# One chip, one core: the heads' skip term as a diagonal product, with moved gate exponentials, state order, fill products in routing and weight pieces between expert blocks

## What is computed

```python
x = x + mamba2(gate(x, f, f, w0, u0, cond))      # state-space layer, 16 heads of 64, state 128
x = x + experts(gate(x, f, f, w1, u1, cond))     # 8 experts, each token goes to two
x = x + attention(gate(x, f, f, w2, u2, cond))   # 16 heads, 4 groups, causal
x = x + ffn(gate(x, f, f, w3, u3, cond))         # 11 slices of 128
```

```python
y = (Y_diag + Y_off) + x_conv * D_skip     # per head and token; D_skip one number per head
y = y * silu(z)
y = y * rsqrt(mean(y * y) + eps) * norm_w
return y @ out_proj.T
```

## Time and profile before

| | |
|---|---|
| median of three runs | 2651.27 us |
| profiled execution | 2644.21 us, its span 2642.5 us |
| mean granted clock of TensorE | 0.938 |
| TensorE busy | 2266.7 us, 86% |
| VectorE busy | 1902.3 us, 72% |
| ScalarE busy | 943.0 us, 36% |
| GpSimd busy | 684.0 us, 26% |
| DMA | 142.19 MB, 54 GB/s |

### The profile page before, as it was taken

The page is one execution under the profiler, slowest core; times in us unless marked ns, Lnnn a source line. Parts: engine busy times, 40 slices in busy tenths (PEclk is TensorE's granted clock), DMA queues, the critical chain, the costliest instruction groups (busy, mean ns, idle before and its releaser), DMA issues.

```text
span 2642.5 us, 33318 instructions
## 1 busy us (share of the span) xinstructions
PE 2266.7 (86%) x10335; PEld 1713.3 (65%) x10352; DVE 1902.3 (72%) x2875; ACT 943.0 (36%) x1948; POOL 684.0 (26%) x545
## 2 busy tenths in 40 slices
PE   0788879979877599988957889999999998999998
PEld 0344444444446478767746777887887877788886
DVE  8888898889885866566635557787787776566665
ACT  2243342442341332333324334444444444322222
POOL 5433434324342334333331102212212210000000
PEclk9998989989986799989978999999999999999999
DMA  5000001001023331343141100001001101000001
GB/s 201 16 32 32 32 16 48 16 16 48 16 78 143 132 111 64 111 151 111 52 183 33 32 0 32 32 0 40 32 0 40 48 16 62 26 24 24 24 12 64
DMA packets 50502, 142.19 MB, mean 54 GB/s; under 512 B 4768, under 2 KB 4768, under 8 KB 46064
## 3 DMA queue, kind: packets, MB, share of 16 engines
q1 hardware_dynamic: 31872, 89.89, 9.6%
q10 hardware_dynamic: 12864, 32.81, 3.4%
q0 software_dynamic: 5680, 18.62, 2.3%
HBM read 106.95 MB, written 34.34 MB: 53 GB/s over the span
## 4 chain that ended last, share of the span: by engine, by line
PE 43%; issue 29%; POOL 9%; DVE 8%; POOLq 5%; ACT 3%; DMA 2%; ACTq 1%; SPq 0%; DVEq 0%
PE bank L340 9%; PE bank L341 9%; PE bank L342 9%; PE bank L2242 4%; PE bank L2243 4%; PE bank L2244 4%; PE bank L2205 3%; POOLq L486 2%; POOL g_v L487 2%; POOL g_v L494 2%; PE bank L2305 1%; POOLq L512 1%; DVE mw L1739 1%; PE bank L2237 1%; POOLq L509 1%
## 5 line engine op out<-in xcount | busy, mean ns | idle before, releaser
L2079 PE MATMUL bank<-um,w_in 128*128 128x512 f32 x576 | 260.3, 606 | 7.0 <-DVE lm L1463 6.7
L2079 PEld LDWEIGHTS bank<-um,w_in 128*128 128x128 f32 x576 | 108.8, 194 | 136.8 <-issue 125.5
L340 PE MATMUL bank<-u_hi,aw_hi 128*128 (+1 forms) x384 | 159.0, 414 | 14.6 <-DVE k_lo L1830 10.9
L1096 ACT ACTIVATE probs<-bank,nmx 128x128 f32<-128x128 f32 (+3 forms) x256 | 131.8, 527 | 91.0 <-DVE nmx L1849 91.0
L341 PE MATMUL bank<-u_lo,aw_hi 128*128 (+1 forms) x384 | 152.2, 396 | 0.0
L342 PE MATMUL bank<-u_hi,aw_lo 128*128 (+1 forms) x384 | 152.1, 396 | 0.0
L1103 ACT ACTIVATE pt_hi<-bank 128x512 fp32r<-128x512 f32 (+1 forms) x192 | 93.9, 526 | 156.7 <-PE bank L2205 156.7
L2205 PE MATMUL bank<-ident,probs 128*128 128x128 f32 x640 | 93.9, 278 | 54.8 <-DVE pt_lo L1864 35.2
L340 PE MATMUL bank<-u_hi,fw_hi 128*128 128x512 f32 x352 | 136.9, 389 | 0.0
L341 PE MATMUL bank<-u_lo,fw_hi 128*128 128x512 f32 x352 | 136.9, 389 | 0.0
L342 PE MATMUL bank<-u_hi,fw_lo 128*128 128x512 f32 x352 | 136.9, 389 | 0.0
(11 more groups left out here) (383 smaller groups left out, 6260.5 us busy)
## 6 DMA issues: line engine op xcount, KB each, us to landing
m_stage<-in_moe SPq DMA_DIRECT2D x21, 1024.0 KB, 6.4
y_slot<-m_o ACTq DMA_DIRECT2D x39, 256.0 KB, 2.4
g_v<-in_fT SPq DMA_DIRECT2D x18, 512.0 KB, 3.4
gates<-g_v SPq DMA_DIRECT2D x18, 512.0 KB, 2.8
f_stage<-in_ffn SPq DMA_DIRECT2D x11, 768.0 KB, 4.3
u_g<-gates SPq DMA_DIRECT2D x8, 1024.0 KB, 5.7
aw_in<-in_att SPq DMA_DIRECT2D x4, 1280.0 KB, 6.0
w_in<-in_w_in ACTq DMA_DIRECT2D x1, 4640.0 KB, 17.0
```

What stands on the lines that cost most here:

```text
L340: nc.tensor.matmul(out, hi_w, hi_x, start=start, stop=False)
L1096: A(probs[:, h % 2, PR_AT[qb]:PR_AT[qb] + w], S_[bk][:, c0:c0 + w], ACT.Exp, bias=nmx[:, h % 2, qb:qb + 1], scale=SCALE, accum_out=rsum[:, ...
L2079: mm = M(dst[:], w_in[:, k, c0:c0 + P], um[:, k, :], start=(k == 0), stop=(k == KC - 1))
```

## The change

Seven edits: `d_diag` is built on ScalarE in the setup and used on TensorE; VectorE's chain of a pair has other operations; block states and state sums have a new common order; gate exponentials and VectorE's clamp and scans of `third` move by one pair; TensorE issues fill products into a spare bank during routing; the weight splits of an expert are cut into pieces that stand between the steps of the next block, in a branch of their own; and the waits are adapted.

```diff
-            sb("pad_x", [P, D_IN], F32, s)
+            d_diag = sb("d_diag", [P, XC, P], F32, s)
...
+        AT_PREFIX, AT_POSITION, AT_ROWS = 38, 47, 51
...
+        def keep_busy(n):
+            for _ in range(n):
+                nc.tensor.matmul(SPARE[:].rearrange("p (a l) -> p a l", a=TB), ident_b[:],
+                                 causal_b[:].unsqueeze(1).to_broadcast([P, TB, P]), start=True, stop=True)
...
+        STATE_ORDER = [(0, 0), (0, 1), (1, 0), (1, 1), (0, 2), (1, 2)]
...
+            for j in range(XC):
+                A(d_diag[:, j, :], ident[:], ACT.Copy, scale=col("d_skip", j)).then_inc(setup_act, 1)
...
-                    if j == 1:
+                    if j == 2:
                         gate(mamba_pair(b, 2), 1)
-                    if j == 6:
+                    if j == PAIRS - 1:
                         gate(mamba_pair(b, 3), 0)
...
                     with act.If(flags[q] != 0):
                         e = act.value_load(...)
                         act.wait_ge(dn_done, FIRST + j)
-                        split_hi(e, e % 2)
-                    up_tanh(j + 1, (q + 1) % 3)
-                if not (last and q >= 1):
-                    u_hi_copy(j + 2)
+                        split_hi(e, e % 2, (0,))
+                        up_tanh(j + 1, (q + 1) % 3)
+                        split_hi(e, e % 2, (1,))
+                        if not (last and q >= 1):
+                            u_hi_copy(j + 2)
+                        split_hi(e, e % 2, (2,))
+                    with act.Else():
+                        up_tanh(j + 1, (q + 1) % 3)
+                        if not (last and q >= 1):
+                            u_hi_copy(j + 2)
...
-                    i = (TB - 1) * half + tb
+                    i = STATE_ORDER.index((half, tb))
...
-                for half in range(2):
-                    for tb in range(TB - 1):
-                        state_sum(tb, half)
+                for half, tb in STATE_ORDER:
+                    state_sum(tb, half)
...
                     step.inc(V.tensor_tensor(ej[:, P:T], YO[:, P:T], ej[:, P:T], ALU.mult))
-                    V.scalar_tensor_tensor(xj, xj, col("d_skip", j), YD[:], ALU.mult, ALU.add).then_inc(y_read, 1)
+                    dve.wait_ge(zs_done, PAIRS * b + j + 1)
+                    step.inc(V.tensor_tensor(xj[:, 0:P], YD[:, 0:P], zs[:, j, 0:P], ALU.mult))
                     step.wait()
+                    V.tensor_tensor(xj[:, P:T], YD[:, P:T], ej[:, P:T], ALU.add).then_inc(y_read, 1)
                     dve.wait_ge(y_read, PAIRS * b + j + 1)
-                    step.inc(V.tensor_tensor(xj[:, P:T], xj[:, P:T], ej[:, P:T], ALU.add))
-                    step.wait()
-                    dve.wait_ge(zs_done, PAIRS * b + j + 1)
-                    V.tensor_tensor(xj, xj, zs[:, j, :], ALU.mult).then_inc(y_done, 1)
+                    V.tensor_tensor(xj[:, P:T], xj[:, P:T], zs[:, j, P:T], ALU.mult).then_inc(y_done, 1)

                     if j == 0:
                         clamp(third, 0)
-                    elif j == 1:
+                    elif j == 2:
                         clamp(third, 1)
-                    elif j < 4:
-                        scans(third, j - 2)
+                        scans(third, 0)
+                    elif j == 3:
+                        scans(third, 1)
...
+            def next_inner(j, q, last):
+                inner(j + 1, (q + 1) % 3)
+                if not (last and q >= 1):
+                    select(j + 2, (q + 2) % 3)
+                    u_lo_split(j + 2)
...
-                        split_lo(e, e % 2)
-                    glu(j + 1, (q + 1) % 3)
-                    inner(j + 1, (q + 1) % 3)
-                if not (last and q >= 1):
-                    select(j + 2, (q + 2) % 3)
-                    u_lo_split(j + 2)
+                        split_lo(e, e % 2, (0,))
+                        glu(j + 1, (q + 1) % 3)
+                        split_lo(e, e % 2, (1,))
+                        next_inner(j, q, last)
+                        split_lo(e, e % 2, (2,))
+                    with dve.Else():
+                        glu(j + 1, (q + 1) % 3)
+                        next_inner(j, q, last)
...
                 to_tokens(7)
-                pe.wait_ge(xdt_done, XC * b + 7)
-                block_state(0, 2)
                 pe.wait_ge(xdt_done, XC * (b + 1))
-                for tb in range(TB - 1):
-                    block_state(1, tb)
+                for half, tb in STATE_ORDER[2:]:
+                    block_state(half, tb)
...
                 for j in range(PAIRS):
-                    pe.wait_ge(m_ready, 2 * (PAIRS * b + j + 1))
                     if j:
                         pe.wait_ge(y_read, PAIRS * b + j)
+                    M(YD[:], d_diag[:, j, :], xa[:, j, :], start=True, stop=False)
+                    pe.wait_ge(m_ready, 2 * (PAIRS * b + j + 1))
                     for hh in range(2):
                         for tb in range(TB):
                             M(YD[...], xdt[...],
-                              lm[:, j % 2, hh, tb * P:(tb + 1) * P], start=True, stop=True)
+                              lm[:, j % 2, hh, tb * P:(tb + 1) * P], start=False, stop=(tb == TB - 1))
...
+            pe.wait_ge(ob_read, KC * BATCH + 1)
...
                     if a >= 3:
+                        keep_busy({3: 12, 7: 16}.get(a, 0))
                         pe.wait_ge(ut_copied[(a - 3) % 2], (a - 3) // 2 + 1)
                     for kc in range(KC):
                         mm = transposed(UT[a % 3][:, kc * P:(kc + 1) * P], uf1[:, b, kc, o])
                     mm.then_inc(ut_T, 1)
+                    if a >= 3:
+                        keep_busy(2)
...
+            keep_busy(10)
             pe.wait_ge(route_vec, MASK_READY)
...
+            for at in (AT_PREFIX, AT_POSITION, AT_ROWS):
+                pe.wait_ge(dve_step, DVE_MAMBA * BATCH + at)
+                keep_busy(8)
             pe.wait_ge(route_vec, ONEHOT_READY)
...
             mm.then_inc(route_mm, 1)
+            keep_busy(8)
...
             pe.wait_ge(route_vec, TAB_READY)
+            keep_busy(12)
             inputs_T(0, 0, 0)
```

More of the change, by code:

```diff
@@ L326, in network @@
         BC = SM, EB
-        UT, LGP = bank[4:7], bank[7]
+        UT, LGP, SPARE = bank[4:7], bank[7], bank[0]
+        AT_PREFIX, AT_POSITION, AT_ROWS = 38, 47, 51
         UG, UL, DN, TP = bank[0:3], bank[3:6], bank[6], bank[7]
@@ L971, in u_hi_copy, with split_hi @@
                 A(bu_hi[:].rearrange("p k t -> p (k t)"), TP[:], ACT.Copy).then_inc(bu_hi_ready, 1)
-            def split_hi(e, slot):
-                for p in range(M_PIECES):
+            def split_hi(e, slot, pieces=range(M_PIECES)):
+                for p in pieces:
                     act.wait_ge(m_staged[p], 16 * (e + 1))
@@ L1531, in state_sum @@
                     if tb:
-                        dve.wait_ge(state_done, 2 * (TB - 1) * b + i)
+                        dve.wait_ge(state_done, 2 * (TB - 1) * b + STATE_ORDER.index((half, tb - 1)) + 1)
                         step.inc(V.tensor_tensor(state[:, tb, o].rearrange("p (h d) -> p h d", h=8),
@@ L1677, in _ @@
             each(V.tensor_reduce(nb[:, 0, :], cmp_, AX.X, ALU.add))
+            assert route.n == AT_PREFIX, route.n
             each(V.tensor_tensor_scan(nb[:, 1, :], ones[:, 0:E], nb[:, 0, :], 0.0, ALU.mult, ALU.add))
@@ L1687, in _ @@
                 each(V.tensor_reduce(posf[:, 0, k, :], rtmp[:], AX.X, ALU.add))
+            assert route.n == AT_POSITION, route.n
             each(V.tensor_scalar(posf[:, 1], posf[:, 0], 63.5, 1.0 / P, ALU.subtract, ALU.mult))
@@ L1700, in _ @@
                                       ALU.is_equal))
+            assert route.n == AT_ROWS, route.n
             each(V.tensor_tensor(oh_j[:], choices(1, NBLK), rconst("iota", NBLK).unsqueeze(1).to_broadcast([P, 2 * NT, NBLK]),
@@ L2161, in _ @@
                 to_tokens(7)
-                pe.wait_ge(xdt_done, XC * b + 7)
-                block_state(0, 2)
                 pe.wait_ge(xdt_done, XC * (b + 1))
-                for tb in range(TB - 1):
-                    block_state(1, tb)
+                for half, tb in STATE_ORDER[2:]:
+                    block_state(half, tb)
                 pe.wait_ge(ct_ready, b + 1)
                 for j in range(2):
-                    pe.wait_ge(state_done, 2 * (TB - 1) * b + (TB + j))
+                    pe.wait_ge(state_done, 2 * (TB - 1) * b + STATE_ORDER.index((1, j)) + 1)
                     sums(j)
@@ L2172, in _ @@
                 pe.wait_ge(bc_copied, 2 * TB * (b + 1))
+                pe.wait_ge(setup_act, 4 + 2 * KC + 2 * XC)
                 for j in range(PAIRS):
-                    pe.wait_ge(m_ready, 2 * (PAIRS * b + j + 1))
                     if j:
                         pe.wait_ge(y_read, PAIRS * b + j)
+                    M(YD[:], d_diag[:, j, :], xa[:, j, :], start=True, stop=False)
+                    pe.wait_ge(m_ready, 2 * (PAIRS * b + j + 1))
```

(1 more changed line is left out.)

## The result

The changed kernel took 2612.83 us (median of four runs, 2612.03 to 2615.82) where the kernel before took 2651.59 beside it: a ratio of 0.9857, 95% interval 0.984 to 0.9874. The forecast was 2614. The span of the profiled execution fell from 2642.5 to 2610.2 us.

A forecast was written before the change was run, and what follows sets the result against it. It took VectorE's order and its waits to set the pair loop, with neither TensorE nor VectorE alone bounding the state-space stage. State-space 15, routing 7 and experts 15 sum to 37 us off 2651.3: median 2614, range 2594 to 2634.

The forecast's parts named there:

- The pair loop's term: State-space stage: shorter VectorE chain and moved gate exponentials gain 3.8 us per sequence, 15 us in all (4 to 26).
- its new wait for TensorE: Pair loop: VectorE idles 6.4 us for TensorE at pairs without gate work and pair 0; net of 1.9 before, -4.5.
- The collision: Pair loop: moved clamp and scans, and pair 0's shorter chain, run beside GpSimd's products, costing 2.0 us per sequence.
- I take 3.8: From loop to sequence: of 4.2 us gained, 3.8 remain, mostly where TensorE waited 2.09 for the next sequence's step sizes.
- Routing: Fill products bring TensorE to full clock; nine token tiles take 1.71 us each for 2.45; gain 7 us.
- the losing case: Routing: if the clock stays down despite the fills, a tile takes 3.3 us, a loss of 7.7.
- Rival A: Routing: the fills do not hold the clock, -7.7 for +6.9, total gain 22, median 2629; chance 0.17.
- The expert term: Expert switches: weight pieces cut between the next block's steps let TensorE start earlier; gain 15 us (7 to 24).
- I expect the clock to stay ... 6: Experts: at three of five isolated switches idle under 2 us keeps the clock, about 2 us each, 6.
- Rival B: Pair loop: the diagonal at half clock eats the gain; stage gains 0 to 4, total 24, 2627; chance 0.15.
- D: Skip term has no effect, waits move to the next sequence's start; 22 to 26 left; chance counted within B's 0.15.
- C: Slower: the diagonal on every pair's path costs 57 us over 32 pairs, net +35, 2686; chance 0.02.

The follow-up runs named there:

- run 1: Changed kernel with VectorE's old four operations per pair and no diagonal product, the moved gate work and state order kept: 2618.62 us.
- run 2: Changed kernel with gate exponentials, clamps, scans and block-state order as in the kernel before, the diagonal product kept: 2638.28 us.
- Runs 1 and 3: run 1, and the changed kernel with only the old order of the block states, gate moves and diagonal kept: the latter 2610.45 us.
- run 6: Changed kernel without the two fill products inside each routing tile, all other fills kept: 2612.38 us.
- run 7: Changed kernel with all three expert weight pieces copied and subtracted ahead of tanh and gate product, as before the change: 2620.57 us.
- run 8: Changed kernel with the first two expert weight pieces ahead of tanh and gate product, the third behind the input split: 2602.22 us.
- run 10: On top of run 8, 34 fill products ahead of attention's first combine and 30 behind its first query projection: 2604.07 us.
- run 11: The changed kernel once more, unaltered, on the same chip as a repeat of run 8: 2609.19 us.

## Why the prediction was right, and where it was not

**The pair loop's term was too low (3.8 a sequence forecast, 6.9 measured in the third).** The working of the loop itself held as a sum: 4.2 forecast, 58.9 to 54.6 = 4.3 measured, but the parts differ, and that they cancel is luck. In the second sequence VectorE's busy time in the loop fell by 1.4 us (50.0 to 48.6) where 5.2 - 2.0 = 3.2 was forecast, and its idle time by 3.0 (8.8 to 5.8) where 5.5 - 4.5 = 1.0 was: its new wait for TensorE, put at 6.4, was 2.5. The waits for ScalarE were worth their 5.5: gate moves and state order alone shorten the loop by 5.8, and 0.2 of these waits is left then (run 1); with the diagonal 2.3 to 2.4 stay. The diagonal was to give 5.2 - 4.5 = 0.7 in the loop; it costs 1.5 to 1.7 there (VectorE's wait for TensorE is 7.3 with the diagonal alone and 1.9 in the kernel before), and gives 1.9 (alone) to 2.8 (with the moves) ahead of the next loop. The collision was there too: the scans L449 take 5.7 us for 4.7, beside GpSimd. The step that failed is the next one, "I take 3.8", which let the wait for step sizes in the next sequence eat part of the gain and counted nothing else in front of the loop. That wait barely moved (2.09 to 1.82), and the part ahead of the sums became 2.6 shorter. Two things are in it: the state order, 0.7 to 0.8 as forecast, which I had counted inside the loop; and TensorE at full clock in the first block states, 1.94 us at a granted clock of 1.00 where the kernel before took 3.37 at 0.55 for the same four records. In the kernel before:

```profile
524.90 3.37 PE L2155 MATMUL bank<-state,b_tok 128*128 128x512 f32 x4
```

and in the changed kernel:

```profile
511.53 1.94 PE L2182 MATMUL bank<-state,b_tok 128*128 128x512 f32 x4
```

In the last three sequences these records take 3.2 to 3.6 us in both profiles of the kernel before and in run 2, and 1.9 to 2.0 in all nine profiles with the changed kernel's code. Runs 1 and 3 have both: 1.9, 3.2 and 2.8 without the diagonal, 3.1, 1.9 and 1.9 with the old state order, and the part ahead of the sums goes with it (91.5, 93.1 and 92.8; 92.6, 91.0 and 91.0). The idle time right ahead, 2.4 us, is the same in all of them. So in these sequences full clock was seen only with the gate moves, and every time only with all parts together; why stays open. This time ahead of the loop is what the step left out.

**Routing was right in size and mechanism**: 7.9 and 7, tiles of 1.71, and 3.3 us in tiles at half clock ahead of them, the number of the losing case, which cost nothing, because ScalarE's next copy of a transpose waits for a store until 805.44. Rival A fell, and run 6 shows that without the two fills in each tile the clock falls as it says, at a price of 2.1 us and not A's 14.6 (four of the nine tiles still run at full clock, and none has fills to pay for): the trace's rows at 0.50 were good evidence, and with the two fills in each tile the clock held at 1.00 all the same.

**The expert term was too high (15; 11.0 by run 7, about 6 over all profiles).** Isolated switches gave 14.3, more than the 11 forecast, though 3.9 of it lies in the first block, whose length varies. "I expect the clock to stay ... 6" failed: TensorE idles 1.86 us and the blocks behind gain 3.3 together, one of them losing. The single-block expert cost 8.5 for 7, and the two blocks behind it returned 3.0, not 5.2: -5.5 for -1.8. The first price of the new order is thus the dependency that run 8 removes: a piece that the next product needs was put behind an operation that waits for the product before it.

**What was not foreseen: the profile of before was not typical of its runs.** It lay 7 us under its median, and I took the same 7 for the kernel after; there the profiled execution and the median agree within 1 us (2612.03 and 2612.83). Two places carry the scatter. (a) The first four expert blocks take 45.3 to 46.6 us or 48.3 to 49.4 in fourteen profiles of eleven kernels, with one of each for the kernel before. In the long ones of the new order (five) VectorE's scans in the second block wait for GpSimd and run beside it, and TensorE waits for the split behind them, as here in run 6:

```profile
877.28 4.32 DVE L449 TENSOR_TENSOR_SCAN g_s<-decay,g_s 128x512 f32<-128x512 f32 x2 [1.30 <-POOL g_v L495]
```

(2.33 us in the changed kernel, unhindered). With the old order of the pieces VectorE's three subtractions in the first block are what collides: 10.30 us in run 7, 7.79 and 8.88 in the two profiles of the kernel before, 6.70 undisturbed. (b) Attention takes 925.2 to 933.9 us. Up to the first copy of the values all profiles agree within 2 us; the stretch to the second is 78.3 to 86.6, with a granted clock of 0.86 to 0.90 in those up to 83.1 and 0.84 to 0.86 in those over 85. In the two profiles of the kernel before attention is 925.5 and 928.9, in the two of the changed kernel 933.1 and 931.4, in run 8 and its repeat 925.2 and 926.6, and 932.7 with the old pieces. Whether the change, by when the stage begins, makes the long form likelier stays open: the clock goes with it, but run 10, which raised it ahead of the stretch, did not settle which is the cause.

So the median came out right by luck, because errors cancelled: 11 us too little in the state-space stage, 4 to 10 too much in the experts, 5 to 8 not counted in attention. In the profiles the gain is 32.3 us where 37 was forecast, in the medians 38.8, and the difference is the 7 us by which the first profile lay low, less the 0.8 by which the later one did. Rival B had the right mechanism, the diagonal on TensorE's path, and the wrong consequence: it overlooked that the loop's loss comes back where VectorE was the later of the two. D, by which the skip term gives nothing, comes nearest to runs 1 and 2 on that term; its total missed since the moves gave more than all of the stage was to give (24.3 us in run 1, for 15). C was far off, as its rows said.

## What to carry to other kernels

When work moves from one engine to another inside a loop, look for its worth also where the two meet next: here the loop became longer and the sequence a little shorter. When a block of copies is cut into pieces to let dependent steps through, find for every piece who needs it and what that consumer's own predecessor is, for the rarest case too; one expert with a single block ate 8.5 us of what the other switches had earned. And before a sum is made against one profile, look how far it lies from the median: take a second profile, since the difference may lie in stages that the change never touches.

## What was not expected of the hardware

In tiles of four transposes and eight records of narrow logits products TensorE had no idle time at all, and its granted clock still fell from 2.4 to 1.2 GHz between the fourth tile and the fifth (run 6); with two 512-wide bf16 products added to each tile it stayed at 2.4 GHz through all nine (changed kernel). The same two in each of the four tiles before, at 1.2 GHz, left it there. And 34 fills at full clock took 7.5 us of a 13.3 us wait for a DMA: filling half of an idle stretch left the clock of the next 20.9 us at 0.83 (without fills 0.70, 0.71 and 0.84, run 8, run 11 and the changed kernel's first profile), and the time of the stretch to the first copy as it was.
